# Attentions of a four-layer kernel: queries and keys padded to 32 rows per row group by DMA, maxima and exponentials over two banks

## The reference, cut to what matters

```python
x = x + tanh(g_xattn[0]) * L0_xattn(ctx, layernorm(x), b, itok)     # 16 heads of 8, keys masked by position
x = x + tanh(g_ffn[0])   * L0_ffn(layernorm(x))                     # 8 experts, top 2
x = x + tanh(g_xattn[1]) * L1_xattn(layernorm(x), ctx, lens)        # depooling, no softmax
x = x + tanh(g_ffn[1])   * L1_ffn(layernorm(x))                     # five dense layers
x = x + tanh(g_xattn[2]) * L2_xattn(ctx, layernorm(x), fk, fk)      # 8 heads of 16, projected q, k, v
x = x + tanh(g_ffn[2])   * L2_ffn(layernorm(x))                     # 8 experts
x = x + tanh(g_xattn[3]) * L3_xattn(layernorm(x), ctx)              # 16 heads of 8, 256 keys: ctx and own
x = x + tanh(g_ffn[3])   * L3_ffn(layernorm(x))                     # 8 experts
# each attention: softmax(q k^T + mask) v per head, 128 queries of one batch at a time
```

## Time and profile before

| what | value |
|---|---|
| median of 3 runs | 1326.7 us (1324.65 to 1330.88) |
| span of the profiled execution | 1321.6 us |
| its own time | not recorded apart; the median lies 5.1 us above the span |
| attention of layer 0 | 0 to 168.9 us |
| attention of layer 2 | 602 to 732 us |
| attention of layer 3 | 960 to 1228 us |
| TensorE busy | 1159.9 us (88%) |
| VectorE, ScalarE, GpSimd busy | 829.9, 543.4, 296.4 us |
| mean granted TensorE clock | 0.877 of full |

### The profile page before, as it was taken

How to read it: one execution, slowest core, us unless ns; L and a number is a source line. 1 busy time by engine, 2 the same in 40 slices (tenths; PEclk the granted TensorE clock), 3 DMA queues, 4 the chain that set the end, 5 groups by cost and what they waited for, 6 DMA issues and landing times.

```text
span 1321.6 us, 24304 instructions
## 1 busy us (share of the span) xinstructions
PE 1159.9 (88%) x9317; PEld 905.2 (68%) x9317; DVE 829.9 (63%) x1836; ACT 543.4 (41%) x963; POOL 296.4 (22%) x544
## 2 busy tenths in 40 slices
PE   4888999999999499997898998999558999999888
PEld 3666767777777477775676676777356778777655
DVE  4687458788887843333566579999834465551555
ACT  1455544333333233331334676667203455553412
POOL 3223011232221222225363013323320011100100
PEclk9989589999999599998899799999755697885989
DMA  4100000322100200000100024120000000000152
GB/s 153 50 3 3 3 24 27 106 82 70 70 25 1 88 1 0 1 0 33 34 3 3 16 56 115 49 88 32 1 1 2 11 3 3 3 3 2 36 197 95
DMA packets 23009, 49.33 MB, mean 37 GB/s; under 512 B 2800, under 2 KB 6000, under 8 KB 22768
## 3 DMA queue, kind: packets, MB, share of 16 engines
q1 hardware_dynamic: 22176, 46.99, 11.0%
q10 hardware_dynamic: 720, 0.80, 0.2%
HBM read 46.21 MB, written 1.25 MB: 36 GB/s over the span
## 4 chain that ended last, share of the span: by engine, by line
PE 69%; DVE 16%; issue 5%; ACT 5%; POOL 3%; DMA 1%; POOLq 0%; DVEq 0%; SPq 0%; ACTq 0%
PE bank L411 11%; PE bank L158 10%; PE bank L159 10%; PE bank L160 10%; PE bank L436 5%; PE bank L420 3%; DVE NM L490 3%; PE bank L1339 2%; PE bank L1536 2%; PE bank L1340 2%; PE bank L2106 2%; PE bank L374 2%; ACT EE L461 2%; PE bank L1899 2%; PE bank L2113 1%
## 5 line engine op out<-in xcount | busy, mean ns | idle before, releaser
L490 DVE TENSOR_REDUCE NM<-bank 128x2 f32<-128x512 f32 (+1 forms) x224 | 144.0, 685 | 135.3 <-PE bank L411 135.3
L411 PE MATMUL bank<-KT,QT 8*128 8x128 f32 (+2 forms) x1792 | 167.0, 333 | 47.0 <-DVE NM L490 20.3
L461 ACT ACTIVATE EE<-bank 128x512 f32<-128x512 f32 x224 | 121.5, 595 | 184.0 <-PE bank L420 183.8
L411 PEld LDWEIGHTS bank<-KT,QT 8*128 8x128 f32 (+2 forms) x1792 | 139.3, 229 | 83.5 <-issue 36.1
L420 PE MATMUL bank<-QT,KT 10*128 10x128 f32 (+1 forms) x1792 | 168.8, 336 | 1.8 <-ACT EE L461 1.7
L1316 ACT ACTIVATE SG<-bank,VC 128x512 f32<-128x512 f32 x128 | 88.2, 689 | 151.2 <-PE bank L160 151.2
L420 PEld LDWEIGHTS bank<-QT,KT 10*128 10x128 f32 (+1 forms) x1792 | 140.0, 231 | 7.2 <-issue 5.2
L1323 DVE SCALAR_TENSOR_TENSOR TT<-bank,VC,SG 128x512 f32<-128x512 f32 x128 | 96.0, 750 | 48.5 <-ACT SG L1316 45.3
L1376 ACT ACTIVATE SG<-bank,VC 128x512 f32<-128x512 f32 x128 | 87.8, 688 | 64.6 <-PE bank L160 62.3
L1393 DVE TENSOR_TENSOR HP<-SG,HP 128x512 fp32r<-128x512 f32 x128 | 95.7, 766 | 18.6 <-ACT HP L1381 15.9
L1233 POOL TENSOR_TENSOR ACC<-ACC,TM 128x512 f32<-128x512 f32 x48 | 65.4, 1364 | 181.8 <-DVE TM L1219 181.2
(11 more groups left out here) (258 smaller groups left out, 2425.7 us busy)
## 6 DMA issues: line engine op xcount, KB each, us to landing
CBS<-cw SPq DMA_DIRECT2D x96, 256.0 KB, 4.6
RAW<-in_w SPq DMA_DIRECT2D x8, 768.0 KB, 4.4
RAW<-in_w SPq DMA_DIRECT2D x8, 512.0 KB, 3.7
RAW<-in_w SPq DMA_DIRECT2D x4, 704.0 KB, 4.4
CTX<-in_ctx SPq DMA_DIRECT2D x4, 512.0 KB, 9.4
FK<-in_fkrow SPq DMA_DIRECT2D x1, 1024.0 KB, 4.7
RAW<-in_w SPq DMA_DIRECT2D x8, 128.0 KB, 2.7
out<-X SPq DMA_DIRECT2D x4, 256.0 KB, 2.3
```

Source lines behind the costliest of these rows:

```text
L411: ins = pe.matmul(self.K.PS[i][:, c:c + 128], qt1[32 * u:k, h:h + 128], kts1[kb][32 * u:k, h:h + 128], start=True, stop=True)
L461: act.activation(self.EE[:, b % 2, 2 * p + i, :], self.K.PS[2 + i][:, :], ACT.Exp).then_inc(sig("ee").sem, 1)
L490: dve.tensor_reduce(out, src, AX.X, ALU.max, negate=True).then_inc(sig("m1").sem, 1)
```

## The change

Four things are done together, in all three attentions.

1. A strip has 32 rows in every score matmul. First scores use rows 0 to 30 of each row group, second scores 0 to 31. The data rows of a head are spread evenly (every fourth or second partition), the rows between hold zeros, row 1 holds ones in the query tile and the mask or nothing in the key tile, row 31 holds ones in the key tile and the negated maximum in the query tile. The constant rows are written once per buffer by `constant_rows` (GpSimd, once VectorE).
2. The widening goes. Queries and keys are made compact, 128 columns, turned or projected once, copied once (`QC`, `KQ`), and a DMA on the SP queue (`sp_rows`, `sp_queries`) places them in the strips. The keys of layer 0 come from device memory in that form, 4 batches a load (`sp_keys`), and so do masks. `KT` of layer 2 has 16 slots, keys of layer 3 lie in 4 extra slots of `KT0`.
3. Banks 0 and 1 become one tile `SA`, banks 2 and 3 `SB`. One VectorE instruction takes the maxima over 1024 columns, one ScalarE instruction the exponentials. In `Attn3` one first-score matmul has 256 moving columns (both key blocks) instead of two with 128.
4. Work moves: the normalisation of `x` goes from VectorE to GpSimd (`pool_normal`), the output bias of layers 2 and 3 is added to `X` by GpSimd beforehand, the mask tiles of layer 2 (`pool_masks`) go, the order within the stages is changed (the transpose of `x` first), input loads are spread over the first stages, and the small weights are prepared in stages 8 and 9.

```diff
-        self.PS = [ctx.enter_context(nc.psum_tensor(f"bank{i}", [128, 512], F32)) for i in range(8)]
+        self.SA, self.SB = (ctx.enter_context(nc.psum_tensor(f"banks{i}", [128, 1024], F32)) for i in range(2))
...
+    def pool_normal(self, n, slot, over, dst, src):
+        pool.wait_ge(*self.sig("stats")(n))
+        pool.tensor_scalar(rs[:, 1:2], mv[:, 0:1], -1.0, 1.0, ALU.mult, ALU.mult).then_inc(*po.up())
+        pool.tensor_scalar(rs[:, 0:1], mv[:, 1:2], over, over * LN_EPS, ALU.mult, ALU.add).then_inc(*po.up())
+        pool.wait_ge(*po.now())
+        pool.tensor_tensor(rs[:, 0:1], rs[:, 0:1], self.HALF[:, 0:1], ALU.pow).then_inc(*po.up())
+        pool.wait_ge(*po.now())
+        return pool.tensor_scalar(dst, src, rs[:, 1:2], rs[:, 0:1], ALU.add, ALU.mult)
...
+    def sp_rows(self, row, src, sem):
+        return self.K.nc.sync.dma_start(row.rearrange("p (g t) -> p g t", g=self.NG), src).then_inc(sem, 16)
+    def sp_queries(self, b, src):
+        return self.sp_rows(self.QT[0:128:self.step, b % 4, :], src, self.K.sig(f"q{b % 4}").sem)
...
-                    k = 32 * u + HD + (1 if self.masked else 0)
-                    ins = pe.matmul(self.K.PS[i][:, c:c + 128], qt1[32 * u:k, h:h + 128], kts1[kb][32 * u:k, h:h + 128],
-                                    start=True, stop=True)
+            if self.NG == 2 and m == 2 and (do1 or do3):
+                ins.then_inc(sig("part").sem, 1)
+                self.parted += 1
+                pe.wait_ge(*sig("part")(self.parted))
+            if do1 and m % self.NB == 0:
+                for i in range(2):
+                    u, g, _ = self.places(p, i)[m]
+                    r = slice(32 * u, 32 * u + 31)
+                    out = K.SA[:, 512 * i + 128 * m:512 * i + 128 * m + wide]
+                    ins = pe.matmul(out, self.QT[r, b1 % 4, 128 * g:128 * g + 128], moving(r, 128 * g), start=True, stop=True)
...
-        for i in range(2):
-            act.wait_ge(*sig("s2")(n + i + 1))
-            act.activation(self.EE[:, b % 2, 2 * p + i, :], self.K.PS[2 + i][:, :], ACT.Exp).then_inc(sig("ee").sem, 1)
+        act.wait_ge(*sig("s2")(self.fills(b) + p + 1))
+        act.activation(self.EE[:, b % 2, 2 * p:2 * p + 2, :].rearrange("p i k -> p (i k)"), self.K.SB[:, :],
+                       ACT.Exp).then_inc(sig("ee").sem, 1)
...
+        dve.wait_ge(*sig("s1")(self.fills(b) + p + 1))
+        dve.tensor_reduce(out, src, AX.X, ALU.max, negate=True).then_inc(sig("m1").sem, 1)
...
# Attn2 and Attn3, SP queue, every stage:
+                sp.wait_ge(*sig("kqc")(s + 1))
+                if s >= 4:
+                    sp.wait_ge(*sig("s2")(H.fills(s - 3)))
+                H.sp_rows(self.KT[0:128:2, s, :], self.KQ[:, s % 2, 0, :], sig(f"keys_in{s % 4}").sem)
+                H.sp_queries(s, self.KQ[:, s % 2, 1, :])
+            if 0 <= b2 < NBAT:
+                H.sp_largest(b2)
...
# Attn3, TensorE:
-                for g in range(4):
-                    ins = pe.matmul(B[:, 128 * g:128 * g + 128], self.WQ[:, 128 * g:128 * g + 128], f[:, 0:128], start=True,
-                                    stop=True)
+                for g in range(2):
+                    ins = pe.matmul(B[:, 128 * g:128 * g + 128], K.wt("Wqkv", 128 * g, 128 * g + 128), f, start=True, stop=True)
```

More of the change, by code:

```diff
@@ L192, in setup @@
[L192 to L197, removed]
@@ L210, in setup @@
[L210 to L218, removed]
@@ L287, in rows, with constant_rows @@
     def rows(self, ap):
         return ap.rearrange("p (h r) -> p h r", r=32)
[L290 to L297, removed]
-        pool.wait_ge(*po.now())
[L299 to L307, removed]
+    def constant_rows(self, eng, dst, n, col):
+        one = self.K.cp("ones").unsqueeze(1).to_broadcast([128, n, 128])
+        return eng.tensor_scalar(dst.rearrange("p (n k) -> p n k", k=128), one, col, 1.0, ALU.mult, ALU.mult)
@@ L314, in fills, with places @@
+    parted = 0
     def fills(self, n):
-        return 2 * self.NP * n
-    def fill1(self, p, part):
+        return self.P * n
+    def places(self, p, i):
         if self.NB == 2:
[L321 to L329, removed]
@@ L358, in pool_keys @@
[L358 to L363, removed]
+            return [(2 * (p // 2) + i, 2 * (p % 2) + m // 2, m % 2) for m in range(4)]
+        if self.NG == 2:
+            return [(2 * (m // 2) + i, m % 2, 0) for m in range(4)]
@@ new lines, in places, with weights @@
+        return [(2 * p + i, m, 0) for m in range(4)]
+    def weights(self, b, h, kb):
+        x, g = (h % 4 + 2) % 4, h // 4
+        i = x % 2
+        if self.NB == 2:
+            p, m = 2 * (x // 2) + g // 2, 2 * (g % 2) + kb
+        elif self.NG == 2:
+            p, m = 0, 2 * (x // 2) + g
+        else:
+            p, m = x // 2, g
+        return self.EE[:, b % 2, 2 * p + i, 128 * m:128 * m + 128]
+    def sp_rows(self, row, src, sem):
+        return self.K.nc.sync.dma_start(row.rearrange("p (g t) -> p g t", g=self.NG), src).then_inc(sem, 16)
@@ new lines, in sp @@
+        for s in range(0, self.LAST + 1):
+            b2 = s - 2
+            if s == 4:
+                self.early.sp()
+            if s < NBAT:
+                sp.wait_ge(*sig("kqc")(s + 1))
+                if s >= 4:
+                    sp.wait_ge(*sig("s2")(H.fills(s - 3)))
+                elif s == 0:
+                    sp.wait_ge(*sig("qc")(1))
+                H.sp_rows(self.KT[0:128:2, s, :], self.KQ[:, s % 2, 0, :], sig(f"keys_in{s % 4}").sem)
+                H.sp_queries(s, self.KQ[:, s % 2, 1, :])
+            if 0 <= b2 < NBAT:
+                H.sp_largest(b2)
@@ L1878, in pe @@
                 read_a.append(sig("ft")(s + 1))
-            if 0 <= b2 < NBAT:
-                H.pe_largest(b2, A[:, 384:512])
-                read_a.append(sig("nmt")(b2 + 1))
+            H.pe_scores(0, b1, moving, b3, keys)
+            if s < NBAT:
+                for r in read_b:
+                    pe.wait_ge(*r)
+                pe.wait_ge(*sig("ft")(s + 1))
+                for i in range(2):
+                    pe.matmul(B[:, 0:128], ws[:, 256 * i:256 * i + 128], fc[:, 128 * i:128 * i + 128], start=(i == 0), stop=(i == 1))
+                pe.matmul(B[:, 128:256], K.wt("Wtgt"), f, start=True, stop=True).then_inc(sig("kq").sem, 1)
+                read_b = [sig("kqc")(s + 1)]
             if 0 <= b4:
@@ L2133, in pe @@
                 read_b = [sig("on")(b4 + 1)]
+            scores(3)
     def act(self):
```

861 lines of the change are left out of this document (448 added, 413 removed).

## The result

The changed kernel takes 1277.3 us (median of 4 runs, 1266.3 to 1281.2) against 1326.7 (1324.7 to 1330.9): ratio 0.961, 95% interval 0.956 to 0.966. Forecast were 1224 us and a range of 1185 to 1275: the median lies 2.3 us above that range, while the ratio applied to 1326.7 gives 1274.6, at its edge. The profiled execution has a span of 1279.8 us, 41.8 under the 1321.6 of before; its mean granted clock is 0.901 (0.877 before).

What follows compares the result with a forecast made beforehand. Few-row score matmuls were taken to hold TensorE's clock down, with VectorE bounding layer 0. Terms: 1321.6 - 63 - 2 - 36 - 2 = 1218.6 us of span, plus 5.1, say 1224 us; range 1185 to 1275.

Steps and rivals of the forecast that it cites:

- Rows and clock: All attentions: the clock follows working array rows, so 31 or 32 rows give 1.00 once both scores overlap.
- Rival 1: All attentions: the clock does not follow rows and slow stages lose only instructions; 1282 us, chance 0.10.
- about half of the gain: Whole kernel: the share of the forecast gain of 103 us put down to the clock.
- Layer 3: Layer 3's attention: stages with both scores at 10.1 us, phase 202 to 203 us against 268; -65, -63 taken.
- Layer 0: Layer 0's attention: -24 from VectorE work taken out and -12 from the start, together -36 us.
- 19.10 - 1.45 = 17.65 in three stages, 5.9 each; with the idle of before 6.5: Layer 0's stages: VectorE's busy time over three stages falls 1.45 us, idle kept, giving 6.5 us each against 7.0.
- paced by GpSimd's constant rows and SP's waits: Layer 0's start: the stages after the first scores come 6 us apart, against some 9.
- Layer 2: Layer 2's attention: no gain in the stages, about -2 us in all, bounds -5 and +8.
- The chain through SP: Layer 2's stage: a loop through SP's issues and the maxima's DMA takes 6.2 us, the 6.21 of before.
- the start, forecast at -2: Layer 2's start: GpSimd's constant rows, 5 us, replace widening and masks, about -2 us in all.
- Rival 3: All attentions: placing DMAs land late behind loads; gain used up at 4.2 us late, 1368 us at 5; chance 0.05.
- rival 4: All attentions: maxima and handovers taken as hidden bind, 1.5 us a stage more over 32 stages; 1272 us, chance 0.10.

Runs made afterwards that it cites:

- e1: The kernel before with score matmuls over all 32 rows of their strip, added rows zero, nothing else changed: 1253.1 us, ratio 0.941.
- e2: The changed kernel with first scores over 9 rows and second scores over 10, most products left out: 1402.2 us, ratio 1.054 to the kernel before.
- e9: The changed kernel with seven unused 128-column full-array matmuls in each of layer 0's stages: ratio 0.969 to the kernel before, layer 0's phase 173.6 us.
- e7: The changed kernel with six unused 128-column full-array matmuls ahead of the scores in layer 2's stages: ratio 0.960 to the kernel before.
- e11: The changed kernel with layer 0's depooling matmul, and ScalarE's copy for it, back ahead of the second scores and exponentials: 1261.3 us, ratio 0.947.
- e12: e11 with layer 0's next queries also turned right behind the first scores: ratio 0.952 to the kernel before, layer 0's phase 148.5 us.
- e8: The kernel before with 32-row score matmuls, maxima and exponentials over two banks, and unused 512-column matmuls at the attentions' starts: 1235.5 us, ratio 0.934.
- e3: The changed kernel with each 256-column first-score matmul of layer 3 split into two of 128 columns: ratio 0.966 to the kernel before.

## Why the prediction was right in its mechanism and wrong by 53 us

The profiled execution, the slowest of the four, is 61 us over its forecast, the median 53.

**Rows and clock: right.** The step that went against the page of the Trainium skill holds. The Trainium skill, "TensorE: Matmul & The Clock Gate", Part 1, ties the gate to busyness and idle gaps; by that rule e1 would have changed nothing and e2 nothing. They changed the time by -6% and, against the changed kernel, +10%. Rival 1 is out. The share given to it was too small: forecast "about half of the gain" of 103; measured with e1, 69 us of span, more than the whole gain of 42.

**Layer 3: right, 21 us too much.** The steady stage was forecast at 10.1 us and is 10.35; the maxima take 1.22 us as forecast, but the chain runs over TensorE and the exponentials (L386 released by L430 for 15.7 us in 990 to 1156), not over VectorE at 2.52 us a fill. VectorE's timeline after:

```profile
1060.54 1.22 DVE L456 TENSOR_REDUCE NM<-banks 128x4 f32<-128x1024 f32 x1 [0.78 <-PE banks L386]
...
1063.21 1.23 DVE L456 TENSOR_REDUCE NM<-banks 128x4 f32<-128x1024 f32 x1 [0.96 <-PE banks L386]
...
1065.67 1.22 DVE L456 TENSOR_REDUCE NM<-banks 128x4 f32<-128x1024 f32 x1 [0.82 <-PE banks L386]
```

The mis-sized terms: from the barrier to the first turn of maxima 27.3 us against 23.8; the fifteen stages after it 164.9 against 154.7, mostly because the lower clock lasts up to three stages longer than I let it (13.75, 12.92 and 11.03 us at clocks of 0.50, 0.76 and 0.94, where 10.1 was taken for each); and 31.6 against 24 for the end, at a clock of 0.68, which I had taken as full. This end is also what makes the phase vary: in the seven unaltered runs it took from 25.4 us at a clock of 0.93 (e9) to 37.1 at 0.54 (e7).

**Layer 0: wrong, 28 us.** The step that failed is "19.10 - 1.45 = 17.65 in three stages, 5.9 each; with the idle of before 6.5". The idle time of before was carried over as if only work were taken out. The diff also moves the depooling matmul behind the second scores, and I gave that move no line. It puts scores, depooling matmul, VectorE's read and maxima in a row, and e11 shows its price, 11 us, the clock that it cost included. The turn that shares a bank with the output step is worth about 3 more (e12, near the spread of the phase), and the stage of 12.6 us where I took 6 is SP's queue: the "paced by GpSimd's constant rows and SP's waits" of the prediction, mis-sized. The first scores came at 16.9 us, as forecast.

**Layer 2: wrong, 14 us.** The chain through SP was right (forecast 6.2 us, 6.5 measured), and so was that nothing was gained. (The 6.21 us taken for the stage of before was its one longer one; the other steady ones are 6.12.) Two things were missed. First, a TensorE that loses six instructions and waits for a DMA does not keep its clock; the prediction asked of rows only and not of the idle time that it made itself (e7). Here what the same page of the Trainium skill says of busyness agrees with the trace: 78% busy, clock 0.92, against 90% and 1.00 before. Second, the start, forecast at -2: from the barrier to the first turn it took 25.5 us instead of 17.3. SP's timeline, with GpSimd's instruction ahead of it:

```profile
602.36 3.67 POOL L274 TENSOR_SCALAR KT<-CP 128x4096 f32<-128x4096 f32 x1
```

```profile
606.18 2.55 SPq L1925 DMA_DIRECT2D KT<-NEG  x4
608.83 0.61 SPq L321 DMA_DIRECT2D KT<-KQ  x1
```

The constant rows, then four issues of mask rows, then the keys: TensorE's first scores start at 611.9, 13.5 us past the barrier, against 10.0 before. (SP waits there for VectorE's mask too; that instruction, 16x128, took 2.38 us beside GpSimd's and ended at 606.1 with it.) The four issues were in the diff and not in the sum. The other 4.7 of the 8.2 us pass between first scores and first turn, at a clock of 0.53 in 597.7 to 624 us (0.82 before, in 602 to 623.3), where the second batch's scores wait 1.75 us for their queries' DMA.

**The rivals.** No single one came true. Rival 3 (placing DMAs in the path) names layer 2's loop and layer 0's late second turn, at a small part of its price; its sign, first scores released by a DMA in every stage, did show in layer 2; rival 4's number, 1272, is near, but its mechanism, 1.5 us a stage in all attentions, is not: layer 3's stages are within 0.25 us of the forecast.

**Open.** What in the order of work makes the clock fall again and again in the changed kernel's layer 0 and not in e11's was not isolated; the longest wait of TensorE in the stages was 2.7 us there and 1.4 in e11 (43 to 130 us). Why layer 3's last 31 us run at 0.68 after the change (0.54 to 0.93 over the runs), and e1's last 22.6 at 1.00, was not tried.

## What to carry to other kernels

Matmuls that use few rows of TensorE can cost twice their time by the granted clock alone: where a long stretch is busy and yet clocked at 0.5 to 0.7, pad the contraction with zero rows before restructuring anything. Ask of every other part of a change how much full-array work it removes and where it makes TensorE wait, since the clock can take the gain back. And when work is taken out of a stage, draw the new loop with its order on each queue, moved instructions first; the old idle time doesn't carry over.

## What the runs showed of the hardware that I had not expected

- Rows that hold only zeros count for the clock (e1). With 9 and 10 rows a strip the clock stayed at the 1.2 GHz level for 185 us of 93% busy TensorE, and didn't rise once (e2).
- Unused full-array matmuls shorten a phase where they lie under a wait (e7: 136.1 us against 137.9 to 146.7, the whole kernel no different; e8, at the starts of the phases: 9 us in all) and lengthen it where they lie in the loop (e9: 11 us).
- Among seven executions with the same layer 3, its last stages took 25.4 us at a clock of 0.93 in one and 37.1 at 0.54 in another: one profile of such a stretch says little.
- A matmul of 256 columns over 31 rows took 399 ns and one of 128 columns 283 ns beside it at the higher level, 668 and 436 ns at the lower (with 9 and 10 rows); one wide or two narrow ones made no difference to a stage (e3).
- One reduction over two banks took 1.22 us, two in a row over one bank each 1.29.
